# Two transformer layers and a linear attention on one core: a new order of the layer steps over five slots instead of six

## The reference, cut to what matters

```
x = x + ga * linear_attention(layernorm(x) * (1 + ca) + sa)
h = layernorm(x) * (1 + cb) + sb
for l in range(2):
    q, k, v = split(shift(h) @ wqkv[l])
    q, k = rotary(l2norm(q) * qs, l2norm(k) * ks)
    h = h + local_attention(q, k, v) @ wo[l]
    a, g = split(norm(shift(h)) @ w1[l] + b1[l])
    h = h + (a * gelu(g)) @ w2[l] + b2[l]
x = x + gb * h
```

## Time and profile before

| | us |
|---|---|
| median of 3 runs | 3239.49 |
| lowest, highest | 3235.77, 3242.86 |
| the profiled execution | 3241.86 |
| its span, first to last instruction | 3240.0 |

### The profile page before, as it was taken

One profiled execution on the slowest core, in us unless ns is written; L12 is line 12 of the kernel. 1 busy time (PEld: TensorE's weight loads), 2 busy tenths in 40 slices (PEclk: granted clock), 3 DMA queues, 4 the chain that ended last, 5 costly groups with the idle time before them and its releaser, 6 DMA issues.

```text
span 3240.0 us, 85044 instructions
## 1 busy us (share of the span) xinstructions
PE 3149.2 (97%) x25452; PEld 2440.9 (75%) x25452; DVE 2658.3 (82%) x8314; ACT 2144.6 (66%) x5372; POOL 2574.6 (79%) x2892
## 2 busy tenths in 40 slices
PE   6999999699999999999999999999999999999998
PEld 3777677477777777777777777777777777777777
DVE  5999999578777777777777788888888888888884
ACT  3666666367777776767677777776777676767674
POOL 3999999687777777777777778888888888888884
PEclk8999999899999999999999999999999999999999
DMA  7211111000000000000000001111111111111111
GB/s 234 64 48 48 47 50 45 27 22 24 24 25 24 25 24 25 24 24 25 24 24 25 24 25 37 37 37 38 37 38 37 38 37 37 38 37 37 38 37 30
DMA packets 148856, 125.07 MB, mean 39 GB/s; under 512 B 18356, under 2 KB 144808, under 8 KB 148144
## 3 DMA queue, kind: packets, MB, share of 16 engines
q1 hardware_dynamic: 141840, 108.56, 11.0%
q10 hardware_dynamic: 6560, 11.02, 1.1%
HBM read 77.49 MB, written 42.02 MB: 37 GB/s over the span
## 4 chain that ended last, share of the span: by engine, by line
PE 92%; POOL 3%; issue 2%; DVE 1%; ACT 1%; ACTq 0%; DMA 0%; DVEq 0%; POOLq 0%; SPq 0%
PE bank L559 33%; PE bank L760 19%; PE bank L768 10%; PE bank L566 9%; PE bank L733 7%; PE bank L712 6%; PE bank L627 2%; PE bank L645 2%; POOL shared L1303 1%; PE bank L607 1%; PE bank L610 1%; PE bank L638 1%; PE bank L656 1%; PE bank L746 0%; PE bank L675 0%
## 5 line engine op out<-in xcount | busy, mean ns | idle before, releaser
L760 PEld LDWEIGHTS bank<-zT,W 128*128 128x128 f32 x5632 | 667.2, 192 | 137.5 <-issue 135.1
L559 PE MATMUL bank<-WQKV,xT 128*128 128x512 f32 x1536 | 744.3, 607 | 11.2 <-ACT xT L784 6.5
L1339 POOL TENSOR_TENSOR rnorm<-clamped,HALF 128x8 f32<-128x8 f32 x256 | 420.4, 1642 | 411.9 <-DVE clamped L1168 405.4
L760 PE MATMUL bank<-zT,W 128*128 128x128 f32 x5632 | 671.0, 275 | 14.0 <-issue 12.0
L1352 POOL TENSOR_TENSOR shared<-shared,share_of 128x512 f32<-128x512 f32 x512 | 585.6, 1171 | 59.0 <-DVE shared L1203 59.0
L934 ACT ACTIVATE shared<-shared,negmax 128x256 f32<-128x256 f32 x1024 | 505.6, 495 | 26.8 <-DVE negmax L1187 25.2
L559 PEld LDWEIGHTS bank<-WQKV,xT 128*128 128x128 f32 x1536 | 263.4, 191 | 221.8 <-issue 214.0
L1165 DVE TENSOR_REDUCE sums<-rotary_work 128x8 f32<-128x512 f32 x256 | 175.6, 686 | 285.3 <-ACT rotary_work L904 281.0
L1203 DVE COPY_PREDICATED shared<-BEYOND,shared 128x256 f32<-128x256 int32 x512 | 399.2, 791 | 0.0
L1187 DVE CUSTOM_DVE_ANT_0 shared<-bank,MASK 128x256 f32<-128x256 f32 x1024 | 366.2, 420 | 0.1
L1362 POOL TENSOR_TENSOR shared<-shared,IDENT 128x256 f32<-128x256 f32 x512 | 362.1, 728 | 0.0
(11 more groups left out here) (157 smaller groups left out, 6649.7 us busy)
## 6 DMA issues: line engine op xcount, KB each, us to landing
X<-xl_rows SPq DMA_DIRECT2D x128, 128.0 KB, 2.1
X<-in_x SPq DMA_DIRECT2D x64, 128.0 KB, 2.1
x_tiles<-ax SPq DMA_DIRECT2D x64, 128.0 KB, 1.7
xl_rows<-axl SPq DMA_DIRECT2D x64, 128.0 KB, 1.7
XS<-xl_rows SPq DMA_DIRECT2D x128, 64.0 KB, 2.1
xm_rows<-X SPq DMA_DIRECT2D x128, 64.0 KB, 1.6
xs<-xm_rows SPq DMA_DIRECT2D x128, 64.0 KB, 1.8
xl_rows<-X SPq DMA_DIRECT2D x64, 128.0 KB, 1.7
```

The costliest lines, as they stand in the source:

```text
L559: mm = nc.tensor.matmul(held(tile, key)[:, 0:cols], lhsT[c], rhs[c], start=(c == 0), stop=(c == len(lhsT) - 1))
L760: mm = nc.tensor.matmul(held(tile, key)[:, k * P:(k + 1) * P], W1[:, tile.l, c, at:at + P], zT[:, c], start=(c == 0), stop=(c == KC - 1))
L1339: G.tensor_tensor(rnorm[q][:], clamped[q][:], HALF[:].to_broadcast((P, LH)), ALU.pow).then_inc(done[f"root_{key}"], 1)
```

## The change

The table `ORDER_L` is another one, for the same steps: a tile now passes slots 0 to 4 (before: 0 to 5). On ScalarE `age_k` stands directly ahead of `keep_k`. The bank tables are others, too. `ORDER_A` and all steps are as they were. The diff, cut to ScalarE's list; the lists of the other engines and the banks change in the same way:

```diff
@@ ORDER_L @@
...
-    "ACT": [(1, "square_q"), (0, "age_k"), (4, "norm"), (5, "gelu"), (0, "keep_x"), (1, "keep_q"), (0, "square_k"),
-           (4, "affine"), (1, "exp0"), (1, "exp1"), (1, "exp2"), (1, "exp3"), (0, "keep_k"), (0, "keep_v"), (2, "keep_o")],
+    "ACT": [(1, "square_q"), (1, "age_k"), (1, "keep_k"), (4, "gelu"), (0, "keep_x"), (1, "keep_q"), (1, "keep_v"),
+           (3, "norm"), (0, "square_k"), (3, "affine"), (2, "keep_o"), (1, "exp0"), (1, "exp1"), (1, "exp2"), (1, "exp3")],
...
```

20 lines of the change are left out of this document (10 added, 10 removed), and 16 rows, old and new, of tables (BANK_L, ORDER_L).

## The result

The changed kernel takes 3374.07 us, the median of 4 runs (3364.05 to 3378.91); beside it the kernel before took 3240.74 us (3235.77 to 3242.86, 4 runs). The ratio is 1.041, 95% interval 1.0395 to 1.0424. The forecast was 3343 us, 3285 to 3400: the right direction and inside the range, 31 us too low. The profiled execution of after is the fastest of its four, 3364.05 us, with a span of 3362.2 us.

A forecast was written before the change was run, and what follows sets the result against it. TensorE's own work, 20.12 us a slot, bounds the kernel; a new ring adds 0.93 us in 125 slots: 3241.86 + 116 - 12.9 = 3345 us, 3343 on the median's footing, range 3285 to 3400 us.

The forecast's parts named there:

- The bound: Layer stage of the kernel before: TensorE's own work sets the pace, 20.12 us a slot.
- the ring: Layers: dependencies from `weigh` through `keep_o`, exponentials, `root_x`, `norm`, `turn_z` back to `weigh`; 21.05 us a slot (20.25 to 21.75).
- the third: First exponential to `sum_q`, through VectorE's `invert2`, `add_o`, `invert3`: claimed 5.4 us, bounds 4.6 and 6.1.
- Rival (a): VectorE's copies not slowed by shares, 0.43 us each: slot 20.25 us, about 3243 us; chance 0.05.
- rival (c): VectorE's copies slowed fully, 1.21 us each: slot 21.75 us, about 3430 us; chance 0.09.
- The turns of the loop: Fourteen in the layers; VectorE's taken as ScalarE's 1.62 us, so no difference; 22 us either way left open.
- The ends: Filling and emptying of the layers: one emptying slot fewer, 12.9 us gained; filling slots counted as unchanged.
- The signs: Profile after: TensorE busy about 93%, waiting about 0.9 us a slot; `turn_z` every 21.0 us; table load between `keep_o` and exponentials.
- rival (d): ScalarE's table load: a drain of about 1380 ns at every set change; slot 22.43 us, about 3515 us; chance 0.01.
- The second ring: Leaves the ring after `rotate_q`, through gates, `narrow`, transposes and `project_k` to `turn_z`: 20.65 us a slot.

The follow-up runs named there:

- the first experiment: Changed kernel with `keep_o` moved behind `exp0` on ScalarE: 3241.17 us (3238.60 to 3243.69, 10 runs), ratio to the kernel before 1.0011.

## Why the prediction came out as it did

*The bound and the ring: right.* The slot of before is TensorE's 20.12 us; the new ring was named step by step, and the first experiment opened it and took the loss of the full slots with it, all but 0.04 us. Its mean was forecast at 21.05 us and measured at 21.04.

*That mean is right for a wrong reason.* Term by term, in the long slot shown:

| term of the sum | forecast | measured |
|---|---|---|
| `weigh` to `keep_o` | 2.02 | 2.01 |
| `keep_o`, table load | 1.91 | 1.91 |
| first exponential to `sum_q` | 5.4 | 5.81 (short slots 4.69) |
| `sum_q` to `scale_q` | 2.99 | 2.98 |
| `scale_q` to end of `root_x` | 5.90 | 5.72 |
| `norm` to `turn_z` | 1.05 | 0.97 |
| `turn_z` to `weigh` | 1.78 | 2.01 |
| sum | 21.05 | 21.41 |

The step that was wrong is the third. I took the copies beside shares as slowed in proportion, 0.95 and 0.85 us, between the 0.43 and 1.21 of the earlier trace rows. No copy on the ring takes such a time: they are 1.31 and 1.12, or 0.43 and 0.63. The two ends of the bound, 4.6 and 6.1, are near the two real cases, 4.69 and 5.81, and the value between them fits the mixture of about two thirds long and one third short by luck. Rival (a), a ring of 20.25 us, was nearly true for the short slots, and rival (c), 21.75, lay nearer to the long ones (21.3 to 21.6) than the forecast's 21.05. The earlier trace rows could have told it: 1.21 - 0.43 = 0.78 is less than a share's 1.14, so a copy that starts inside a share and ends just after it fits as well as a slowdown does.

Smaller: a share between `scale_q` and a diagonal takes 1.00 by starts, not the 1.14 that I took from four in a row (copies of VectorE lay beside those); `turn_z` to `weigh` is 0.23 us longer than in the earlier trace rows, where TensorE comes to it without a wait.

*The turns of the loop: a term put at nothing.* I counted fourteen turns; twelve show, six a layer. I took VectorE's turn to be ScalarE's 1.62 us and the difference as none. It is 4.4 us in the first layer (22.1 over 5) and 2.5 in the second (12.6 over 5), all on the ring. The forecast had 12 x 0.93 = 11 us for these slots; they cost 39.9, so 29 us were missing, more than the 22 that I had left open. The trace of before held a hint that I did not show, VectorE's `sum_q` at a turn:

```profile
1067.43 0.69 DVE L1165 TENSOR_REDUCE sums<-rotary_work 128x8 f32<-128x512 f32 x1 [3.90 <-ACT rotary_work L904]
```

3.90 us of idle time, put down to ScalarE, which is the last to come there, where 2.3 us are usual. Over all turns it is 3.9 to 4.1 us in the first layer and 3.3 to 3.6 in the second. That bounds VectorE's turn at that place in that kernel, and it was this bound, not ScalarE's turn, that belonged into the sum's range; even so the first layer's 4.4 us lie above it.

*The ends: one part right, one missed.* Forecast -12.9, one emptying slot, with the filling slots unchanged; measured -19.1 by the distances of `turn_z`. At which end it was they can't say, since `turn_z` stands one slot nearer to a tile's start now. `turn_x` opens a tile in both kernels, so it can. Its matmuls (count, shortest, median and longest in ns, first and last start in us) in the kernel before, in the changed one, and in the run with `keep_o` behind `exp0`:

```profile
L566 PE MATMUL bank<-IDENT,X x128: 272/273/417, 589.5 to 3158.3; 128*128 128x128 f32 x128
L566 PE MATMUL bank<-IDENT,X x128: 272/273/421, 588.0 to 3288.1; 128*128 128x128 f32 x128
L566 PE MATMUL bank<-IDENT,X x128: 272/273/418, 588.2 to 3171.4; 128*128 128x128 f32 x128
```

and the fifth of them, before and changed:

```profile
667.97 0.42 PE L566 MATMUL bank<-IDENT,X 128*128 128x128 f32 x1
654.84 0.27 PE L566 MATMUL bank<-IDENT,X 128*128 128x128 f32 x1
```

From the last one to the end of the span it is 81.7 us before, 74.1 in the changed kernel and 69.1 with `keep_o` behind `exp0`. So the emptying slot of 12.9 us was priced rightly, as 12.6 us once the ring is open; in the changed kernel, whose last slots still run on the long ring, 7.6 are left of it. What the forecast had wrong is "unchanged": the four slots in which the pipeline fills take 66.9 us instead of 78.5, 11.6 less. How much of that is fewer waits and how much TensorE's clock, no run separates: in these slots the granted clock is 0.74 to 0.91 before and 0.85 to 0.95 in the changed kernel. Another 1.5 us lie ahead of the layers. Together that is 20.8 us, 1.6 more than by `turn_z`, since other slots count as the full ones. The run with the cut ahead of `keep_p0` saves 12.6 us at the emptying and 11.4 at the filling.

*The account.* Forecast on the spans 116 - 12.9 = 103 us; measured 122.2. The difference, by the distances of `turn_z`: +29 by the turns, -6 by the ends, and about -4 by 123 slots instead of 125 at 0.913 instead of 0.93 us. So the total came out as near as it did partly because these misses have different signs. The medians are another 11 us apart than the two profiled runs (133.3 against 122.2); that is within the runs of the changed kernel, which scatter by 15 us, those of before by 7. Whether the mixture of slots differs from run to run is not shown, since one run of the kernel was profiled.

*The signs.* Waits at `turn_q` (0.46 and 0.56 us in two slots, behind `scale_q`) and ScalarE's `norm` behind `root_x`: as said. A wait of TensorE at `turn_z` hardly shows, 1.1 us in all of 1000 to 1900 us against 30.3 us at `turn_q`; of the 0.9 us a slot the rest lies in matmuls that last longer in the records. First exponential 1.31 us after the end of `keep_o`, with the table load between: as said. The load began 0.02 us after `keep_o` and there was no drain, so rival (d) is out. (The Trainium skill, ScalarE: Activation LUTs, What ACT_TABLE_LOAD costs, has that drain; the trace of after does not agree, with 1.31 us for the whole switch, 1530.34 minus 0.02 to 1531.63.) "21.0 us in both layers" was right for the mean (21.1 and 21.0) and wrong for each slot. TensorE's share was to fall to 93% and fell to 95%: the same 25452 matmuls are shown busy for 3208.9 us instead of 3149.2, and some last longer in the records (`turn_z` 0.33 instead of 0.27 us). The chain of waits shows a ring more surely than that share.

*The second ring* exists, but the wait in its slots is at `turn_q` for `scale_q`, not at `narrow` for the gates as I had it. Its 20.65 us were 20.8 in slots with slow copies, and under 20.12 in the others.

## What to carry to other kernels

Follow every order of instructions round to itself one slot later and add it up; a ring that is 1 us too long costs it in every slot, and the cure may be one step moved over its neighbour (here a copy and the table load behind it). Two engines that shut each other out must be costed by who starts first, with the two ends as two cases and not with a value between, and a tiny delay may be worth more than it costs. The cut of a loop's list acts like an instruction of several microseconds on that engine (2.4 to 5.5 us on VectorE here): put it where the engine has that much idle time behind it, and test again when another ring has become shorter.

## What the runs showed of the hardware

- A predicated copy of VectorE (128x256) takes 0.42 to 0.44 us with no share beside it in the changed kernel. When it starts 0.032 us or more inside a share of GpSimd (1.04 us), it ends 0.30 to 0.32 us after the share, 332 times out of 332, and takes 0.62 to 1.32 us. When it starts ahead of the share or up to 0.033 us behind it, it keeps its 0.42 to 0.47 us, and the share takes 0.15 to 0.30 us more. I had expected a slowdown of both in proportion.
- VectorE's turn of the loop leaves it idle for 2.4 to 5.5 us, by the place of the cut, the layer and the kernel (4.4 and 2.5 us in the changed kernel, 5.1 and 3.4 with `keep_o` behind `exp0`, 5.4 and 3.3 with the cut ahead of `sum_q`, where the kernel before has 3.9 to 4.1 and 3.3 to 3.6), while ScalarE's is 1.62. What makes the length is open; no run here separates it.
- With such a contest a pipeline need not have a single period: like slots take 20.3 or 21.3 us in an order that looks random. That its times scatter more for it is not shown: four runs of the changed kernel lie within 15 us, but four with the ageing of keys one slot earlier, with 25 short slots of the 111, within 3.5.
